# A transformer decoder layer on one core: which engine copies which head in attention, and the place of three instructions

## The reference, cut to what matters

```python
q = (x @ Wq).reshape(B, T, H, Dh)          # B=4, T=512, H=16, Dh=32
k = (x @ Wk).reshape(B, T, H, Dh)
v = (x @ Wv).reshape(B, T, H, Dh)
scores = jnp.einsum('bthd,bshd->bhts', q, k)
mask = jnp.tril(jnp.ones((T, T), dtype=scores.dtype))
scores = scores * mask
attn = jax.nn.softmax(scores / T ** 0.5, axis=-1)
out = jnp.einsum('bhts,bshd->bthd', attn, v).reshape(B, T, H * Dh)
return out @ Wo
```

## Time and profile before

| what | us |
|---|---|
| median of 3 runs | 1457.94 (1457.32 to 1458.15) |
| the profiled execution | 1456.45 |
| its span in the trace | 1454.7 |
| PE, DVE, ACT, POOL busy in it | 1414.1, 989.0, 699.1, 388.4 |

### The profile page before, as it was taken

One profiled execution on the slowest core, in us unless ns is written; L12 is line 12 of the kernel. 1 busy time (PEld: TensorE's weight loads), 2 busy tenths in 40 slices (PEclk: granted clock), 3 DMA queues, 4 the chain that ended last, 5 costly groups with the idle time before them and its releaser, 6 DMA issues.

```text
span 1454.7 us, 26922 instructions
## 1 busy us (share of the span) xinstructions
PE 1414.1 (97%) x8896; PEld 719.3 (49%) x8896; DVE 989.0 (68%) x2125; ACT 699.1 (48%) x1600; POOL 388.4 (27%) x705
## 2 busy tenths in 40 slices
PE   6999999999999999999999999999999999999999
PEld 3475467457546744444444444444444444444444
DVE  7796688589578868886665675666666666766533
ACT  5794288149428834435335344353353353443432
POOL 1054234305473455421211121221112112212100
PEclk9999999999999999999999999999999999999999
DMA  7563613542455501010100100100001001000011
GB/s 253 135 187 111 183 63 96 144 122 88 148 153 186 203 19 44 17 34 17 33 18 17 34 17 17 33 16 20 17 17 34 17 17 34 17 17 1 1 59 58
DMA packets 77311, 98.02 MB, mean 67 GB/s; under 512 B 8049, under 2 KB 60785, under 8 KB 76785
## 3 DMA queue, kind: packets, MB, share of 16 engines
q1 hardware_dynamic: 77168, 96.23, 21.5%
HBM read 68.94 MB, written 27.26 MB: 66 GB/s over the span
## 4 chain that ended last, share of the span: by engine, by line
PE 86%; DVE 4%; ACT 4%; issue 4%; POOL 1%; DMA 0%; ACTq 0%; DVEq 0%; POOLq 0%; SPq 0%
PE bank L901 25%; PE bank L903 25%; PE bank L902 25%; PE bank L968 3%; ACT prob L1290 2%; PE bank L989 2%; PE bank L956 1%; PE bank L914 1%; PE bank L1044 1%; PE bank L1029 1%; PE bank L998 1%; PE bank L1039 1%; DVE xt L1606 1%; PE bank L1050 1%; DMA X<-in_x_dram 0%
## 5 line engine op out<-in xcount | busy, mean ns | idle before, releaser
L901 PE MATMUL bank<-xs,G 128*128 128x512 f16 x896 | 339.8, 379 | 2.4 <-issue 1.1
L902 PE MATMUL bank<-xs,G 128*128 128x512 f16 x896 | 339.6, 379 | 0.0
L903 PE MATMUL bank<-xs,G 128*128 128x512 f16 x896 | 339.6, 379 | 0.0
L1752 DVE TENSOR_TENSOR c<-bank,c 128x512 f32<-128x512 f32 x128 | 88.0, 689 | 193.6 <-PE bank L903 193.6
L1368 ACT COPY c<-bank 128x512 f32<-128x512 f32 x192 | 111.2, 579 | 220.9 <-PE bank L903 216.0
L901 PE MATMUL bank<-Wd,hid 128*128 128x512 f16 x512 | 194.1, 379 | 2.8 <-DVE X L1806 2.8
L903 PE MATMUL bank<-Wd,hid 128*128 128x512 f16 x512 | 194.0, 379 | 0.0
L902 PE MATMUL bank<-Wd,hid 128*128 128x512 f16 x512 | 194.0, 379 | 0.0
L764 POOL TENSOR_TENSOR c<-c,m 128x512 f32<-128x512 f32 x64 | 82.3, 1286 | 389.4 <-ACT c L1368 389.4
L1806 DVE SCALAR_TENSOR_TENSOR X<-bank,col,X 128x512 f32<-128x512 f32 x128 | 95.4, 750 | 101.5 <-PE bank L903 101.4
L1290 ACT ACTIVATE prob<-bank,nmx 128x129 f32<-128x129 f32 (+3 forms) x256 | 146.9, 586 | 8.4 <-POOL nmx L779 8.4
(11 more groups left out here) (197 smaller groups left out, 2391.5 us busy)
## 6 DMA issues: line engine op xcount, KB each, us to landing
stack<-qk_dram SPq DMA_DIRECT2D x128, 128.0 KB, 3.3
sc_in<-scale_t SPq DMA_DIRECT2D x30, 384.0 KB
qk_dram<-qk SPq DMA_DIRECT2D x32, 256.0 KB, 3.0
packed_t<-pk_t SPq DMA_DIRECT2D x32, 192.0 KB, 1.9
pk_in<-packed_t SPq DMA_DIRECT2D x30, 192.0 KB
X<-in_x_dram SPq DMA_DIRECT2D x4, 1024.0 KB, 5.7
pk_in<-L_ffn_gate_W_packed_dram SPq DMA_DIRECT2D x16, 256.0 KB, 2.7
pk_in<-n_L_ffn_up_W_packed_dram SPq DMA_DIRECT2D x16, 256.0 KB, 3.1
```

The costliest lines, as they stand in the source:

```text
L901: pe.matmul(o, lhs(0), rhs(0), start=first, stop=False, skip_group_check=onto)
L902: pe.matmul(o, lhs(0), rhs(1), start=False, stop=False, skip_group_check=onto)
L903: return pe.matmul(o, lhs(1), rhs(0), start=False, stop=stop, skip_group_check=onto)
L1752: nc.vector.tensor_tensor(dst[:], bank[at][:], dst[:], ALU.add).then_inc(comb, 1)
```

## The change

Five edits, all in the unit loop:

1. `copied_by_act`: before, ACT copied two heads of tile i = 3 (units 3, 7, 11; three in unit 15) and three of the others. Now it copies two heads of tile i = 2 (units 2, 6, 10, 14) and three of all others, unit 15 among them. DVE copies the rest. The third head of a unit is copied one unit later in the queue, in both engines.
2. `values` of the units 2, 6 and 10 is issued after the fourth `scores` of the next step instead of before it: that score moves ahead, between `recips` and `values`.
3. ACT's first copy of a unit with i = 1 is issued before the fourth exponential instead of after it.
4. POOL's `out_tail` is issued one `shift` earlier.
5. The waits in `turn_read`, `act_copies` and `vector_copies` follow from edit 1.

```diff
         def copied_by_act(u):
-            return 2 if u % TT == TT - 1 and u < UNITS - 1 else 3
+            return 2 if u % TT == TT - 2 else 3
...
                             convert(n * (NB // B) + r, r, 3 * i + j - 7)
-                        if j == 3 and i == 0 and r > 1:
+                        if j == 2 and i == 0 and r > 1:
                             out_tail(n, r - 2)
...
                         if u + 1 < UNITS:
                             scores(n, u + 1, j)
+                        if j == 3 and u > 0 and sooner(u - 1):
+                            values(n, u - 1)
                         turn(n, u, j)
...
                         if j == 2 and u > 0 and sooner(u - 1):
                             recips(n, u - 1)
-                            values(n, u - 1)
...
-                        if j == 3 and u % TT < 2:
+                        if j == 3 and u % TT == 0:
                             turned(n, u, 0)
                             turned(n, u, 1)
-                        elif j >= 2 and u % TT >= 2:
+                        elif j >= 2 and u % TT > 0:
                             turned(n, u, j - 2)
```

## The result

| what | before | after |
|---|---|---|
| median, us (6 runs each) | 1458.05 (1456.49 to 1460.22) | 1463.89 (1462.84 to 1465.34) |
| ratio after / before, 95% interval | | 1.0039 [1.0030, 1.0049] |
| span of the profiled execution, us | 1454.7 | 1462.3 |
| first to 16th `divide` of the four passes, us | 51.86, 51.87, 51.86, 49.41 | 53.29, 53.26, 53.47, 50.79 |

The change makes the kernel 5.8 us slower; the prediction said 5.6 us and 1463.5. A pass, measured from VectorE's first `divide` to its 16th, grew by 1.4 (by 1.6 in the third), and the four together from 205.00 to 210.81, +5.81. That is the whole difference of the medians.

What follows compares the result with a forecast made beforehand. A closed loop of PE and VectorE hand-overs, 13.65 us per four units, bounds the kernel. Terms +1.88 + 0.15 - 0.64 = +1.39 a pass, +5.6 us over four passes, gave 1463.5; range 1456.5 to 1466.5.

Steps and rivals of the forecast that it cites:

- The copies, +1.88 a pass: VectorE's four added 384-column copies, in units 2, 6, 10, 14, each delay what follows by 0.47 us, uncovered.
- The stretch of 5.05: Loop link on VectorE from its repacking copy to the copy of (10, 3), 5.05 us; PE waits for VectorE there.
- The removed copies of 512 columns, 0: VectorE losing the copies of (3, 2), (7, 2), (11, 2) saves nothing: it idled 0.76 for a score there anyway.
- The score's move: Fourth score between `recips` and `values` makes PE leave and re-enter 32-column tiles: costs 0.11 to 0.22 us, taken as 0.20.
- the 2.45: PE link from transposes of (7, 1) to (7, 3), 2.45 us before; expected 2.55 after, +0.15 a pass including unit 3.
- The relief ahead of the repacking copy: VectorE waits less before its repacking copy because ScalarE's first copy comes one exponential earlier: -0.64 us a pass.
- the 0.28 go: VectorE's 0.28 us wait ahead of the repacking copy, in groups with a low half, was expected to vanish entirely.
- The stretch of 1.81: PE link from the transpose of (8, 2) through `values` of unit 7 to the score of (10, 0), 1.81 us.
- The end of a pass: In unit 15 the added copy's delay passes through `values` to the following dense work, with nothing taking it up.
- the first: Rival, faster: PE reaches the transposes of (7, 1) late enough to cover the added copies; -3.6 us, 1454.3; chance 0.14.
- The second: Rival, no change: VectorE is bound by its sum of work, +0.05 us a pass, 1458.1; chance 0.16.
- The third: Rival, slower still: full drains make the score's move cost 0.34 instead of 0.20, +1.7 us, 1465.2; chance 0.10.

Runs made afterwards that it cites:

- k1_copies: Kernel before with only the new split of who copies which head, issue orders unchanged: 1463.04 us against 1457.3, ratio 1.0035.
- x_loop: Kernel before plus an unused 384-column VectorE maximum ahead of the copies of (2, 3), (6, 3), (10, 3), (14, 3): 1462.35 us against 1457.8, ratio 1.0029.
- x_idle: Kernel before plus an unused 512-column VectorE maximum ahead of the copies of (3, 2), (7, 2), (11, 2): 1457.70 us against 1457.8, ratio 0.9995.
- k3: Kernel before with only ScalarE's first copy of units with i = 1 moved ahead of the fourth exponential: 1456.56 us against 1457.7, ratio 0.9995.
- k4: Kernel before with only GpSimd's low half (`out_tail`) issued one shift earlier: 1456.12 us against 1457.7, ratio 0.9989.
- k34: Kernel before with only ScalarE's earlier first copy and GpSimd's earlier low half: 1456.89 us against 1457.3, ratio 0.9995.
- k2_score: Kernel before with only the fourth score moved ahead of `values`, between `recips` and `values`: 1462.6 us against 1457.3, ratio 1.0034.
- k134: Changed kernel without the fourth score's move ahead of `values`: 1461.08 us against 1457.3 for the kernel before, ratio 1.0020.

## Why the prediction was right, and which terms were off

The forecast held in time (1463.5, measured 1463.89) and in its mechanism. Point by point:

- **The copies, +1.88 a pass.** Right. The stretch of 5.05 became 5.50, +0.45 of the 0.47 forecast. In the last group of a pass (13th to 16th `divide`), where little else changes, 10.85 became 11.32, +0.47. k1_copies and x_loop, with x_idle beside them, show that the place is what costs.
- **The removed copies of 512 columns, 0.** Right within what can be told: x_idle puts as much work into that gap, and three of its four passes lose nothing.
- **The score's move and the wait in the 2.45, 2.55 after.** The stretch took 2.58, so +0.13 in unit 7 and -0.03 in unit 3 (2.61 to 2.58). The price of the split was 0.23 where I took 0.20 and set the upper end at 0.22; the wait of 0.10 went as forecast.
- **The relief ahead of the repacking copy, -0.64 a pass.** The reason was right, the size was not. Of "the 0.28 go" only 0.20 went, and the 0.08 in the group without a low half stayed (213.47 to 213.64 in the second pass before, 216.35 to 216.51 after). That makes -0.40 a pass. I had taken 0.08 as what the small operation holds VectorE for; it is 0.16, the distance that is left wherever nothing waits, in the first group of before as in k3, k4, k34 and after. So the real wait was 0.20 with a low half and 0 without. That ScalarE's copy, one exponential earlier, is enough, and that the low half "adds nothing" to it, is what k3 shows, 0.16 by edit 3 alone. What I did not see is that edit 4 would have been enough too (k4), and that edit 3 without it costs 0.10 in the stretch behind.
- **Two links that I held fixed.** The hand-over from the transposes of (7, 3) to their copy grew from 0.64 to 0.70: they follow a 32-column run now, and their record is 0.66 instead of 0.61. The stretch of 1.81 fell to 1.68. In before the last transposes of unit 8 started 0.20 behind the score ahead of them, as the rows below show; in after it is 0.11 (226.96 to 227.07), which fits ScalarE's copies of unit 8: they start at 226.21, 0.61 before PE gets to the transpose at 226.82, and in before at 350.18, 0.06 before it gets to the one at 350.24. Both changes come with edit 2: k2_score has 0.70 and 1.68, k134 has 0.65 and 1.80. So part of the price of the split comes back there, and after's group is only 0.19 longer than k134's.
- **The sum.** By the group of unit 7: +0.13 + 0.06 - 0.01 - 0.13 + 0.01 - 0.20 + 0.45 = +0.31, measured +0.31 by `divide`, three times, and +0.47 in the last group: 1.39 or 1.40 a pass, forecast +1.39. What was off nearly cancels: the relief +0.24 a pass, the transposes' link 3 x 0.06, PE's stretch +0.08 (0.13 + 0.13 - 0.03 and not 0.15), against 3 x 0.13 in the 1.81. That the sum is exact is partly luck: its terms are right to 0.1 or so a group, and 0.2 of the 5.81 is the longer group of the third pass, which no term foresaw.
- **The end of a pass.** Right. After the 16th `divide` nothing took the time up: pass lengths grew by 5.81 and the medians by 5.84. PE waits for the last `divide` as in the earlier trace rows:

```profile
385.85 1.08 PE L989 MATMUL bank<-prob_t,V 128*32 128x128 f32 x32 [0.70 <-DVE c_in L1661]
```

The timeline of PE in before behind the transpose of 350.24, third pass:

```profile
350.38 0.27 PE L956 MATMUL bank<-stack 128*128 128x257 f16 x1
350.58 0.30 PE L968 MATMUL bank<-ident,prob 128*128 128x128 f32 x1
```

The rivals: PE did not reach the transposes of (7, 1) late enough for the copy to find cover; it idled 0.51 for it, 0.15 behind its end, so the first falls. The second falls by x_idle and x_loop. The third has one part that holds: the rule of the Trainium skill ("TensorEngine Tiling (Array Packing)", section Key Properties), that a change of the tiling mode drains TensorE, agrees with the 0.12 on the way out and the 0.10 on the way in. But the full drain as the third rival priced it, with `values` starting after the score's record has ended, did not come: the score starts at 224.12, its record ends at 224.35, and `values` starts at 224.28. Of the 0.34 it would have cost, 0.23 did.

## What to carry to other kernels

Where no engine is full, look for the closed loop of hand-overs and add up its starts: 0.61 us of extra work a group beside it cost nothing in most groups, 0.47 on it cost 0.37, and the page's busy shares were the same in both. Before moving a copy between two engines, ask what its new place delays, and whether it can stand ahead of the next step's work and not behind it. When a loop is shortened, expect another engine to take it over, and read there before the next step: the earlier copy gained in the middle groups only once ScalarE had been relieved as well.

## What the runs showed of the hardware

- Splitting one run of 32-column matmuls by a full one cost 0.23 us: 0.12 to leave the tiles, 0.10 to take them up, and a full-width run of four transposes behind such a run was recorded with 0.66 instead of 0.61 and read 0.06 later by VectorE.
- A waiting engine started 0.15 us after the end of a VectorE copy (222.56 to 222.71), and PE 0.05 to 0.06 after ScalarE's read of its accumulator (346.55 to 346.60, 349.70 to 349.76).
- ScalarE is the faster engine for these copies out of PSUM. By starts, 384 columns took it 0.36 (219.64 to 220.00 in after) and VectorE 0.47 (359.26 to 359.73 in before); 512 columns took it 0.48 (222.18 to 222.66) and VectorE 0.61 (349.40 to 350.01 in before).
